# Gathering raw rows with their statistics instead of stored normalised rows, in a macaron block with two routed expert stages

## What is computed

```
x = x + 0.5 * ffn(layernorm(x), router_W, router_b, W1, b1, W2, b2)
x = x + attn(layernorm(x), ...)
x = x + 0.5 * ffn(layernorm(x), router_W, router_b, W1, b1, W2, b2)

def layernorm(x): (x - mean) / sqrt(var + 1e-5)          # over the 128 values of a row
def ffn(x):
    probs = softmax(x @ router_W + router_b)             # 8 experts
    e = argmax(probs)
    return probs[e] * (relu(x @ W1[e] + b1[e]) @ W2[e] + b2[e])
```

## Time and profile before

| | |
|---|---|
| runs: median (range) | 206.65 us (206.63 to 206.75) |
| profiled execution: first to last instruction (the span) | 213.1 us |
| profiled execution: its own time beside the span | not given apart from the span |
| PE busy | 188.7 us, 89% of the span |
| DVE, ACT, POOL busy | 121.3, 111.6, 122.0 us |
| mean granted PE clock | 0.963 |
| DMA moved | 40.26 MB, mean 189 GB/s |

### The profile page before, as it was taken

The page is one execution under the profiler, slowest core; times in us unless marked ns, Lnnn a source line. Parts: engine busy times, 40 slices in busy tenths (PEclk is TensorE's granted clock), DMA queues, the critical chain, the costliest instruction groups (busy, mean ns, idle before and its releaser), DMA issues.

```text
span 213.1 us, 4561 instructions
## 1 busy us (share of the span) xinstructions
PE 188.7 (89%) x1410; PEld 159.3 (75%) x1410; DVE 121.3 (57%) x516; ACT 111.6 (52%) x328; POOL 122.0 (57%) x186
## 2 busy tenths in 40 slices
PE   4978599997999598898999999998996899999992
PEld 2953269986989597666876588698643899999991
DVE  4858312212212348789897946757531677777762
ACT  2666026644437455778869875131300666666670
POOL 6887456695555526834399704557673154455544
PEclk9976969999999969999999999999999999999998
DMA  5999679764778336169996000001018749676700
GB/s 191 242 381 342 208 249 342 256 197 134 243 174 286 81 85 178 41 259 415 418 410 250 0 2 3 27 28 43 27 63 285 257 165 306 206 264 223 248 27 0
DMA packets 26680, 40.26 MB, mean 189 GB/s; under 512 B 4229, under 2 KB 16296, under 8 KB 25632
## 3 DMA queue, kind: packets, MB, share of 16 engines
q1 hardware_dynamic: 21136, 33.01, 43.9%
q0 software_dynamic: 2496, 4.76, 8.3%
q10 hardware_dynamic: 3024, 2.20, 3.3%
HBM read 10.78 MB, written 14.46 MB: 118 GB/s over the span
## 4 chain that ended last, share of the span: by engine, by line
PE 63%; DVE 13%; issue 9%; POOL 6%; DMA 4%; ACT 2%; another core or an unknown queue 1%; POOLq 0%; DVEq 0%
PE bank L1102 20%; PE bank L1119 18%; PE bank L1238 6%; PE bank L1254 5%; DMA xn_scratch<-xn 3%; PE bank L1095 3%; PE bank L928 2%; DVE stat L1323 2%; POOL xn L581 1%; PE bank L1193 1%; PE bank L1179 1%; DMA Xg<-xn_scratch,srcu 1%; PE bank L1203 1%; DVE x L1558 1%; PE bank L1210 1%
## 5 line engine op out<-in xcount | busy, mean ns | idle before, releaser
L747 ACT ACTIVATE hT<-bank,ewc_own 128x128 f32<-128x128 f32 x184 | 51.6, 373 | 56.7 <-PE bank L1102 38.2
L1102 PE MATMUL bank<-xT,ewc_own 128*128 128x128 f32 x368 | 51.1, 284 | 6.5 <-DVE xT L1455 3.8
L1102 PEld LDWEIGHTS bank<-xT,ewc_own 128*128 128x128 f32 x368 | 46.3, 198 | 9.2 <-issue 9.2
L1119 PE MATMUL bank<-ew,hT 128*128 x368 | 49.4, 278 | 0.0
L1119 PEld LDWEIGHTS bank<-ew,hT 128*128 128x128 f32 x368 | 45.5, 195 | 0.2 <-issue 0.2
L681 POOL DMA_INDIRECT out_dram<-ysb,eqrq x23 | 22.6, 982 | 26.6 <-issue 17.6
L609 POOL DMA_INDIRECT Xg<-xn_scratch,srcu x23 | 22.0, 958 | 15.0 <-PE bank L1102 4.8
L1461 DVE TENSOR_TENSOR ysb<-bank,ewc_own 128x128 f32<-128x128 f32 x23 | 6.7, 289 | 34.1 <-PE bank L1119 26.5
L634 POOL DMA_INDIRECT xnT<-slot_scratch,posu x16 | 15.8, 987 | 13.5 <-DVE ysb L1461 4.3
L928 PE MATMUL bank<-ones_bf 128*128 128x512 bf16 x66 | 19.9, 428 | 3.1 <-POOL ident L499 2.7
L673 POOL DMA_INDIRECT row_scratch<-pay,posu x16 | 15.8, 987 | 10.8 <-DVE posu L1428 6.8
(11 more groups left out here) (239 smaller groups left out, 303.7 us busy)
## 6 DMA issues: line engine op xcount, KB each, us to landing
ewc_own<-ew SPq DMA_DIRECT2D x46, 322.0 KB
row_scratch<-xn SPq DMA_DIRECT2D x8, 1024.0 KB, 10.6
ew<-in_L_ffn_W_dram SPq DMA_DIRECT2D x1, 2048.0 KB, 11.1
slot_scratch<-ysb SPq DMA_DIRECT2D x23, 64.0 KB
ew<-in_L_ffn_W_dram SPq DMA_DIRECT2D x5, 256.0 KB, 9.4
eqrq<-row_scratch SPq DMA_DIRECT2D x18, 70.0 KB
x<-in_L_attn_x_dram SPq DMA_DIRECT2D x4, 256.0 KB, 3.6
xn_scratch<-xn ACTq DMA_DIRECT2D x4, 256.0 KB, 6.2
```

Source lines behind the costliest of these rows:

```text
L747: last = A(hT[:, t.slot, c * P:(c + 1) * P], up_bank(k, c)[:, c * P:(c + 1) * P], ACT.Relu, scale=0.5 if m else 1.0, bias=ewc[t.ahead][:, ...
L1102: last = mm(up_bank(k, c)[:, c * P:(c + 1) * P], ewc[t.ahead][:, c * P:(c + 1) * P], xT[:, t.slot, :], start=True, stop=True)
L1119: last = mm(bank[4 + t.parity][:, 0:D], hT[:, t.slot, c * P:(c + 1) * P], ew[:, bass.ds(e[k], 1), W2_AT + c * D:W2_AT + (c + 1) * D].squee ...
```

## The change

The four stores of `xn` go, and with them `renormalise`, POOL's normalisation of batch 2, `first_shift` and three semaphores. In their place a DRAM tensor `x_scratch` with rows of 130 values holds the raw row, its mean and its reciprocal deviation. SP copies the raw rows from the input to it, DRAM to DRAM, in four DMAs between W1 and W2 of its queue. ACT stores the two numbers of each row from `mv`, in four DMAs among its `take_xn`; POOL's `first_rstd` now writes the reciprocal deviation into `mv`. The gather brings 130 values a row into `Xp`, and DVE normalises the tile into `Xg` (`normal`, until now used in the second expert step alone). ACT's load of W2 for the last three experts waits for the first `ewc` copy. POOL makes its masks before the three `inr` tiles. The fill has a buffer of its own.

```diff
+XW = D + 2
-    xn_scr = nc.dram_tensor("xn_scratch", [TOK, D], f32, kind="Internal").ap()
+    x_scr = nc.dram_tensor("x_scratch", [TOK, XW], f32, kind="Internal").ap()
...
             sp.dma_start(ew[:, :, W1_AT:W1_AT + F], ew1_d.rearrange("e p f -> p e f")).then_inc(ew_in, 16)
+            for g in range(NG):
+                sp.dma_start(x_scr_v[:, g, :, 0:D], x_v[:, g, :, :]).then_inc(x_copied, 16)
             load_w2(sp, range(NE - W2_BY_ACT))
...
-                g.tensor_tensor(out=rstd[:, ts, 0:1], in0=vin[:, n % 2, :, 0:1], in1=mhalf[:, :, 0:1], op=ALU.pow
+                g.tensor_tensor(out=mv[:, ts, 1:2], in0=vin[:, n % 2, :, 0:1], in1=mhalf[:, :, 0:1], op=ALU.pow
                                 ).then_inc(rstd_ready, 1)
...
-            for t in range(POOL_ROWS * GT, (POOL_ROWS + 1) * GT):
-                last = g.tensor_scalar(xn[:, t, :], x[:, t, :], mv[:, t, 0:1], rstd[:, t, 0:1], ALU.subtract, ALU.mult)
-            last.then_inc(xn_by_pool, 1)
...
-                    g.indirect_dma_start(out=Xg[:, k % UNROLL, :], out_offset=None, in_=xn_scr,
+                    g.indirect_dma_start(out=Xp[:, k % UNROLL, 0:XW], out_offset=None, in_=x_scr,
...
-                for b in range(NG):
-                    pool.wait_ge(xn_stored[b], 16)
+                pool.wait_ge(x_copied, 16 * NG)
+                pool.wait_ge(stats_stored, 16 * NG)
                 pool.wait_ge(src_ready, 1)
...
-            def store_xn(g):
+            def store_stats(g):
+                act.wait_ge(rstd_ready, g + 1)
+                act.dma_start(x_scr_v[:, g, :, MEAN_AT:XW], mv[:, g * GT:(g + 1) * GT, :]).then_inc(stats_stored, 16)
...
+            act.wait_ge(ewc_in[0], 16)
             load_w2(act, range(NE - W2_BY_ACT, NE))
             experts(0)
...
                 def turn(k):
-                    if m == 0:
-                        pe.wait_ge(g_in[t.ahead], 16 * (1 + t.round))
-                    else:
-                        pe.wait_ge(xg_ready, t.k + 1)
+                    pe.wait_ge(xg_ready, m * NT + t.k + 1)
...
                 def normal(k):
-                    dve.wait_ge(xp_in[t.ahead], 16 * (1 + t.round))
+                    dve.wait_ge((xp_in if m else g_in)[t.ahead], 16 * (1 + t.round))
...
-                if m == 1:
-                    normal(0)
+                normal(0)
                 take_x(0)
...
                         if n + 1 < NT:
                             take_x(n + 1)
+                        if m == 0 and n + 2 < NT:
+                            normal(n + 2)
```

More of the change, by code:

```diff
@@ L94, in macaron_kernel @@
         xi = sb("xi", [P, T, D])
-        xn = sb("xn", [P, T, D])
+        filler = sb("filler", [P, T * D])
         stat = sb("stat", [P, GT, 6])
@@ L223, in macaron_kernel @@
         rstd_ready = sem("rstd_ready")
[L224 to L227, removed]
+        x_copied = sem("x_copied")
+        stats_stored = sem("stats_stored")
         xnT_ps = sem("xnT_ps")
@@ L597, in _ @@
             g.memset(vx[:, :, :, D:D + 1], 1.0).then_inc(ones_ready, 1)
+            pool.wait_ge(rf_ready, 1)
+            for t in range(T - ROWS_BY_ACT - ROWS_BY_POOL, T - ROWS_BY_ACT):
+                g.tensor_scalar(inr[:, t, :], rowid[:, :], rf[:, t:t + 1], token1[:, t:t + 1], ALU.is_equal, ALU.mult
+                                ).then_inc(inr_by_pool, 1)
             def paced(n):
@@ L620, in move_rows @@
                     if FILL_AT <= k < FILL_AT + FILL_PARTS:
-                        ts = slice((k - FILL_AT) * GT, (k - FILL_AT + 1) * GT)
-                        g.memset(xn[:, ts, :], 1.0).then_inc(fill_ready, 1)
+                        part = T * D // FILL_PARTS
+                        g.memset(filler[:, (k - FILL_AT) * part:(k - FILL_AT + 1) * part], 1.0).then_inc(fill_ready, 1)
                 pool.wait_ge(posu_ready, 1)
@@ L774, in guess_rstd @@
                 A(aguess[:, ts, :], alog[:, ts, :], ACT.Exp, scale=-0.5).then_inc(a_guess, 1)
[L776 to L781, removed]
-            def store_xn(g):
-                if g == POOL_ROWS:
-                    act.wait_ge(xn_by_pool, 1)
-                else:
-                    act.wait_ge(xn_ready, 1 + g - (g > POOL_ROWS))
-                act.dma_start(xn_scr_v[:, g, :, :], xn[:, g * GT:(g + 1) * GT, :]).then_inc(xn_stored[g], 16)
+            def store_stats(g):
+                act.wait_ge(rstd_ready, g + 1)
+                act.dma_start(x_scr_v[:, g, :, MEAN_AT:XW], mv[:, g * GT:(g + 1) * GT, :]).then_inc(stats_stored, 16)
             def row_hits():
@@ L803, in _ @@
             nc.scalar.preload_act_table_set("natural_log_exp_and_others")
-            for g in range(NG):
+            take_xn(0, 0)
+            for g in range(1, NG):
                 take_xn(0, g)
[L806 to L810, removed]
-            store_xn(3)
-            store_xn(POOL_ROWS)
+                store_stats(g - 1)
+            store_stats(NG - 1)
             exponentials()
             row_hits()
+            act.wait_ge(ewc_in[0], 16)
             load_w2(act, range(NE - W2_BY_ACT, NE))
@@ L1333, in pick @@
                 lg_at = pay[:, ts, LG_AT:PW] if m else lg[:, ts, :]
-                scale = pay[:, ts, RSTD_AT:RSTD_AT + 1] if m else rstd[:, ts, 0:1]
+                scale = pay[:, ts, RSTD_AT:RSTD_AT + 1] if m else mv[:, ts, 1:2]
                 dve.wait_ge(logits_ps, m * NG + g + n)
@@ L1367, in row_hits @@
                                     ALU.is_equal, ALU.mult).then_inc(inr_ready, 1)
-            def first_shift(g):
-                ts = slice(g * GT, (g + 1) * GT)
-                dve.wait_ge(rstd_ready, g + 1)
-                v.scalar_tensor_tensor(out=shift[:, ts, 0:1], in0=rstd[:, ts, 0:1], scalar=-1.0, in1=mv[:, ts, 0:1],
-                                       op0=ALU.mult, op1=ALU.mult).then_inc(shift_ready, 1)
             def list_sources():
@@ L1487, in rest_of_rows @@
                         in1=Xp[:, t.ahead, 0:D], op0=ALU.mult, op1=ALU.add))
-                if m == 1:
-                    normal(0)
+                normal(0)
                 take_x(0)
-                if m == 1:
-                    normal(1)
+                normal(1)
                 take_x(1)
-                if m == 1:
-                    normal(2)
+                normal(2)
                 for k in range(NT):
```

12 lines of the change are left out of this document (3 added, 9 removed).

## The result

| | before | after |
|---|---|---|
| median of the runs (range) | 206.64 us (206.12 to 206.75) | 215.85 us (214.7 to 216.75) |
| ratio, 95% interval | | 1.0457 (1.0418 to 1.0495): slower |
| profiled execution: own time, span | span 213.1 (first trace); 206.17, 204.4 (second trace) | 214.7, 213.0 |

The change costs 9.2 us; the forecast was 0.9, the range ended at 210.6. Its first `down` stands at 31.52, against 31.72 in the first trace, so the base that the prediction priced holds. Medians here count every execution of a run; the ratios leave out those in a slower state, so the two need not agree to the last tenth.

A forecast was written before the change was run, and what follows sets the result against it. PE leads from the first `down` at 31.72. The `up` 0.5 us earlier makes it ready at 31.2, but W2 lands at 32.6, 0.9 later: 206.65 + 0.9 = 207.55, forecast 207.6, range 205.3 to 210.6 us.

The forecast's parts named there:

- The place and the path: First expert tile: the first `down`, before at 31.72, would wait for ACT's W2, issued once the first `ewc` copy landed.
- Added, x: 4.1 us: SP's queue between W1 and W2: 2048 pieces of 512 B at 496 a microsecond; bounds 2.8 us and twice 4.1.
- Added, statistics: 3.5 us: ACT's queue: 2048 pieces of 8 B, bounded by 2.7 and 8.6 us, priced near the low end.
- much slower: Rival, small pieces: statistics take 8.6 us, gather starts 27.6, `ewc` copy lands 32.3, W2 37.7; 212.6 us; chance 0.10.
- SP's issue "perhaps 5 later, still before 20.78": SP's issue of W2, ending at 15.12 before, ends perhaps 5 us later, before the list releases the `ewc` copies.
- The first `ewc` copy at 27.2: Behind x, statistics and SP's W2: 25.3 + 4.1 + 3.5 - 2.8 - 3.1 = 27.0, landed at about 27.2.
- W2 at 32.6: ACT's last W2 load: 27.2 + 1.0 + 4.4, first `down` 0.9 us later; low end 30.5, high end 34.6.
- The gather at 22.75 to 23: POOL's first gather starts 1.0 to 1.27 us earlier than 24.02, after the list; tile reaches PE 0.6 to 0.8 earlier.
- My sign for being wrong: First `down` before 31.3, or first gather after 24 with the statistics' DMAs landing last.
- The price of the `xn` stores, 1.2: Ahead of the first gather: stores cost at most 1.2 us beyond the list of sources, all the change can win there.
- The clock: PE near the first `down`: a wait could bring another half-clock stretch, 1 to 2 us; a shorter wait could spare one.
- DVE in the steady tiles: nothing: DVE's 23 normalisations of 0.339 us, 7.8 us in all, stand beside PE's work and add nothing; far end 2.3 us.

The follow-up runs named there:

- e9_from_sbuf: The full change, with the copies of x written from the tile of x in SBUF instead of from the input in DRAM: 216.25 us, 1.0451.
- e11_wait_gather: The changed kernel without copies or statistics, gathers reading the input's rows, ACT's W2 loads held until the second gather has landed: 213.66 us, 1.0382.
- f1_w2_ahead: The full change, with SP also waiting until all of W2 has landed before the third `ewc` copy: 213.11 us, 1.0308.
- e5b_neither: The changed kernel without copies, statistics or ACT's wait, gathers reading the input's rows, one tile's statistics for all: 206.2 us, 0.998.

## Why the prediction was wrong

- **The place and the path** were right: the first `down` decides, it waits for ACT's W2, and that for the first `ewc` copy; the chain after shows it step by step.
- **Added, x: 4.1 us** is the first step that failed. I took the price of pieces of 512 bytes, 496 in a microsecond, because it was the row of the same size. What the row did not share was where a piece begins: 520-byte rows. From 15 to 20 us 1118 packets passed on q1 with statistics beside them, 224 in a microsecond, and 1840 without, 368. By these rates the 2048 pieces take 5.6 us alone and 9.1 beside the statistics, as an estimate, in place of 4.1. My upper bound, twice 4.1, was drawn for another reason (reading and writing DRAM), which e9_from_sbuf does not bear out. Copies and statistics were to end at 21.6 together; the gather that waits for them started at 24.40, so they ended at most 2.8 later.
- **Added, statistics: 3.5 us**: too dear for 8-byte pieces alone, which cost nothing measurable (207.9 against 208.97), and near what they cost beside the copies, where taking them away gives 2.7 us back and ends SP's issue 2.9 earlier. That they slow the copies, and so are dear only beside them, I had not seen. The Trainium skill's "DMA: Bandwidth & Descriptors", section Specifications, has transfers under 512 bytes done as read-modify-write; the price of 8.2 us that I worked out from it is not borne out by the run without copies (1096 pieces at 12.4% of the engines in 5 us, or 1.2 us for 2048, as an estimate). The rival "much slower" came nearest, and by luck: its W2 lands at 37.7, against 38.06, but its gather at 27.6 and its `ewc` copy at 32.3 are some 3 us later than measured, and from that copy to W2 it has the 5.4 us of my forecast, where 8.6 were measured.
- **SP's issue "perhaps 5 later, still before 20.78"**: it ended at 23.69, 8.6 later. What I had called hidden became the head of the chain, 2.05 us of list reading behind it included.
- **The first `ewc` copy at 27.2**: 29.47, from the two sizes above; 2.3 of W2's 5.5 us beyond 32.6.
- **W2 at 32.6**: 38.06. The other 3.1 us are its landing, 7.50 from the last issue where I had used 4.4. I had seen that W2 and the copies would share by halves and put it into the far end, 34.6, not into the forecast. This is the largest single size that was wrong. It is no tail, but a switch: once the first `ewc` copy lands after the first gather, SP's seven next copies stand beside W2 (e11_wait_gather, f1_w2_ahead).
- **The gather at 22.75 to 23**: 24.40, released by the copies, not by the list. My sign for being wrong, a gather after 24 with the statistics landing last, came true in its first half. The price of the `xn` stores, 1.2, is not shown: the second trace of before waits for the list, at 23.44, and where the copies are gone the gather starts at 21.81 and 22.60 behind an earlier list (21.3 and 21.5 instead of 22.3). That a microsecond by the first `down` "goes through to the end" held for the loss (8.42 at the second `down`, 8.49 at the last) and not for a gain, since the sixth gather is paced by PE.
- **The clock**, put at 1 to 2 us as a widening, cost 1.47 behind the wait of 3.69; I had left it out of the sum of the forecast.
- **DVE in the steady tiles: nothing**, right (41.8 us in both, and e5b_neither).

## What to carry to other kernels

Price a DMA by a row whose pieces have the same size and begin on the same multiples: a row that grows from 512 to 520 bytes to hold two more numbers can cost more than the numbers. When a load is made to wait for another, look up which queue's gate opens in the meantime, for the load then lands behind everything that the gate let through. And a gain at the front of a pipeline arrives at its end only if the paced steps behind it move along. Where a forecast hangs on a microsecond, read the wait that it rests on in a second trace of the same kernel.

## What the runs showed that I had not expected

- The 512-byte pieces: 1325 packets in 2 us with rows of 1024 bytes, 770 with rows of 520, engines full in both. Why is not shown.
- 8-byte writes to DRAM pass beside aligned pieces at 12.4% of the engines for 1096, and take 39.4% for 1037 beside unaligned ones in the same rows.
- Copies between DRAM tensors whose rows touch are joined: 1984 packets fewer on the page with rows of 512 bytes.
- Moving one load of 768 KB by 3.4 us, with the same bytes in all queues, was worth 4.7 us (208.97 to 213.66).
